# The first mixer of a two-layer network: the keys' decay differences and products on GpSimd, the head mean at the end of the batch's own body, masked scores ahead of the convolution

## The chip, the core and the metric

One core of a Trainium2 chip runs the whole network in one launch. The time is device microseconds (us) from the start of the program to its end. Engines: PE (TensorE), DVE (VectorE), ACT (ScalarE), POOL (GpSimd), SP (SyncE, which issues most loads). They run side by side, each through its own list of instructions in order, and wait for each other by semaphores.

## The reference, cut to the part that changes

The network is a first mixer, a mixture of experts, a second mixer and a feed-forward block, each followed by a residual sum and a layer norm. Only the first mixer changes. It works on 16 batches of 512 rows by 256 columns, with 8 heads:

```python
xc = _causal_dwconv_silu(x, conv_w)                   # 4 taps
q, kg, v, g = xc @ wq, xc @ wkg, xc @ wv, xc @ wg + bg
gk = jax.nn.log_sigmoid(kg) / NORMALIZER              # decay, 128 columns
k = 1.0 - jnp.exp(gk)
o = _gla(qh, kh, vh, gkh, scale)                      # S = S*exp(gk) + k v ; o = q S, step by step
aug_w = jnp.einsum('bhld,hd,bhld->bhl', qh, aug, kh)
o = o + jax.nn.sigmoid(aug_w[..., None] * vh)
o = (o - mu) * jax.lax.rsqrt(var + LN_EPS)            # mean and variance per row and head
return jax.nn.silu(g) * o @ wout                      # then x = layernorm(x + this)
```

## The kernel before

The first mixer is the function `linear_attention`, whose tiles begin with `gla_`; it fills the first 863 us of the span. A batch has 512 positions, cut into 8 chunks of 64 (`NCH`, `CH`) and, inside a chunk, into 8 pieces of 8 (`NSUB`, `SUB`). Channels lie on the 128 partitions. `G` is the decay summed along each chunk (a scan). Within a chunk scores are formed for a piece of queries against all keys up to it, so each chunk needs eight sets of scaled keys: `kt[..., a, 0:n]` with n = 8(a+1). They are made in three steps per a: a difference of `G` (line 787), an exponential on ACT, and a product with `k` (line 805). An instruction takes all 8 chunks, so it has 64, 128, ... 512 elements per partition. `kt` has two buffers, one for each parity of the batch.

The order on each engine is written by hand, in a function `body(b, u, past, more, far)` per engine. While body b finishes batch b, it also does the last steps of batch b-1 (`past`), the front of batch b+1 (`more`) and the convolution of batch b+2 (`far`). Bodies -1, 0 and 1 come first (`starts`), a loop runs bodies 2 to 13 with two bodies in a turn, and bodies 14, 15 and 16 end it (`ends`). On GpSimd, before, a plain loop runs over the 16 batches: a power -1/2 for the head norm (line 726), one for the row norm (line 729), two stores (lines 732 and 735) and a wait for both of them to have landed.

The steps that the text speaks of, by their names in the code:

- `masked(t)` on DVE (lines 816 to 831): takes two chunks' scores from PE through the causal mask into `A`, and carries the state `S` on by two chunks. `outputs(t)` on PE (lines 1115 and 1118) multiplies `S` and `A`; `outputs(t)` on DVE (line 837) adds them to the sigmoid part in `o`. There are four of each in a batch.
- `head_norm(0)` (lines 843 to 845): mean per head, scale, subtraction. `head_norm(1)` (849, 850): variance, from `squares` on ACT (line 954). Then GpSimd's power. `head_norm(2)` (854) multiplies by silu(g), `head_norm(3)` (857) by the power, into `on`.
- `gates` (773 to 775): decay and the scan into `G`. `differences(0)` (782, 783) makes those for `eR` and `khat`. `products(0)` (794 to 800) makes `qt`, `qhat`, `khat`, `aw`.
- `conv(0)` and `conv(1)` (765, 767): the four taps of one half of the channels.
- `tail(0)` (865): `z`, the output projection plus the residual, from the PSUM banks `pV` and `pW`, then its statistics; `tail(1)` (97): the normalized rows `x1`; `tail(2)` (874): the router's logits `lg`.
- On PE `values(t)` (1075, 1076) multiplies the four row tiles by the joint weight of v and g. `values(0)` writes `pV`, which held the output projection, so it waits until both halves of `z` are read. `scores(0)` of batch b+1, near the end of body b, needs all eight `kt`. The order of PE's instructions is the same in both kernels.

## Time and profile before

| | |
|---|---|
| time, median of 3 runs | 4560.33 us (4553.63 to 4561.02) |
| span of the profiled execution | 4569.0 us, 72542 instructions |
| PE busy | 3959.0 us, 87% |
| DVE busy | 2462.4 us, 54% |
| ACT busy | 1991.1 us, 44% |
| POOL busy | 1091.2 us, 24% |

The profile is one execution on its own. Busy shares are averages over the whole network; what the change does is read inside the first 863 us. A row of the trace gives the start in us from the span's beginning, the length in us, engine, line, operation, output and inputs, how many instructions of that form run in a row, and in brackets how long the engine had been idle before it and what ended that. A window row gives the busy time of PE, PE's weight loads, DVE, ACT and POOL in a stretch, the clock granted to PE as a share of full speed, the share of the DMA engines and GB/s.

### The profile page before, as it was taken

How to read it: one execution, taken by the hardware profiler on the slowest of the kernel's cores; microseconds unless marked ns; L12 is line 12 of the kernel's file. 1: busy time of each engine (PE TensorE's matmuls, PEld its weight loads, DVE VectorE, ACT ScalarE, POOL GpSimd, SP SyncE). 2: the span in 40 equal slices, each digit the busy share in tenths (PEclk: the TensorE clock that was granted, in tenths of full speed). 3: DMA queues.
4: the chain of work that ended last, by engine and by line, in shares of the span. 5: the costliest groups of instructions: out<-in, count | busy, mean ns of one | idle time of the engine just before them, and what ended most of it. 6: DMA issues, size and time to landing. Idle time of an engine off the chain costs nothing.

```text
span 4569.0 us, 72542 instructions
## 1 busy us (share of the span) xinstructions
PE 3959.0 (87%) x23860; PEld 3067.1 (67%) x23860; DVE 2462.4 (54%) x5456; ACT 1991.1 (44%) x4069; POOL 1091.2 (24%) x1686
## 2 busy tenths in 40 slices
PE   6888788598999999994688888888888888779998
PEld 3555555377888888882576767666767677656666
DVE  6888888552222222224567777777777776431111
ACT  5655655111222222212466666666666666432221
POOL 0111111101221222213433333333333332200000
PEclk8888889699999999996799999999999999889999
DMA  1010010244555555552111111111111110011111
GB/s 34 29 42 28 28 42 20 72 139 177 184 184 184 184 184 184 184 172 71 46 32 40 42 38 42 43 42 43 42 42 42 43 42 24 19 57 55 55 55 50
DMA packets 220955, 346.96 MB, mean 76 GB/s; under 512 B 99972, under 2 KB 171908, under 8 KB 202500
## 3 DMA queue, kind: packets, MB, share of 16 engines
q1 hardware_dynamic: 196932, 272.74, 18.7%
q0 software_dynamic: 23760, 71.07, 4.9%
q8 instruction: 122, 2.00, 0.2%
q14 instruction: 141, 1.16, 0.1%
HBM read 276.61 MB, written 68.16 MB: 75 GB/s over the span
## 4 chain that ended last, share of the span: by engine, by line
PE 19%; issue 13%; POOL 10%; DVE 5%; ACT 3%; DMA 2%; SPq 2%; POOLq 0%; another core or an unknown queue 0%; DVEq 0%; ACTq 0%
PE gdr_bank L1320 5%; PE gdr_bank L1311 5%; POOL gdr_vblk L1628 2%; POOL gdr_got L1582 2%; POOL gdr_tblk L1626 2%; PE gdr_bank L2358 2%; DVE gdr_y L1729 2%; PE gdr_bank L2329 1%; SPq L1519 1%; PE gdr_bank L2325 1%; PE gdr_bank L2281 1%; POOL gdr_ssq L1616 1%; PE gdr_bank L2341 1%; DMA blocks_in<-gdr_vblk 1%; DMA gdr_T<-blocks_in 1%
## 5 line engine op out<-in xcount | busy, mean ns | idle before, releaser
L525 ACT ACTIVATE moe_rel<-moe_fc 128x512 f32<-128x512 f32 x284 | 169.6, 597 | 798.4 <-PE moe_fc L490 798.4
L490 PE MATMUL moe_fc<-moe_xT,moe_win 128*128 128x256 f32 x2272 | 503.8, 380 | 1.5 <-issue 0.8
L501 PE MATMUL moe_o<-moe_wout,moe_hT 128*128 128x256 f32 x2272 | 502.0, 379 | 0.0
L490 PEld LDWEIGHTS moe_fc<-moe_xT,moe_win 128*128 128x128 f32 x2272 | 432.8, 191 | 61.2 <-issue 2.1
L501 PEld LDWEIGHTS moe_o<-moe_wout,moe_hT 128*128 128x128 f32 x2272 | 426.3, 190 | 55.1
L549 DVE TENSOR_TENSOR moe_hT<-moe_rel 128x512 f32<-128x512 f32 x284 | 196.7, 693 | 361.2 <-ACT moe_rel L525 361.2
L1729 DVE SCALAR_TENSOR_TENSOR gdr_y<-gdr_bank,gdr_cw,gdr_y 128x511 f32<-128x511 f32 (+2 forms) x384 | 287.5, 749 | 82.4 <-ACT gdr_y L1998 63.6
L2206 PE MATMUL gdr_bank<-gdr_hT,gdr_wqkv 128*128 128x512 f32 x512 | 256.9, 626 | 29.6 <-ACT gdr_qk L2013 24.7
L558 DVE COPY moe_osb<-moe_o 128x512 f32<-128x512 f32 x71 | 49.1, 692 | 424.9 <-PE moe_o L501 424.9
L1311 PE MATMUL gdr_bank<-gdr_hT,gdr_wqkv 128*128 128x512 f32 x512 | 224.1, 596 | 3.1 <-ACT gdr_hT L1329 3.1
L1344 DVE TENSOR_TENSOR gdr_kb<-gdr_bank,gdr_x 128x512 f32<-128x512 f32 x32 | 20.6, 686 | 365.1 <-PE gdr_bank L1320 365.1
L2329 PE MATMUL gdr_bank<-gdr_T,gdr_nAT 128*128 128x64 f32 (+1 forms) x1536 | 199.1, 280 | 0.0
L2358 PE MATMUL gdr_bank<-gdr_wo,gdr_y 128*128 128x256 f32 x512 | 156.3, 473 | 48.7 <-ACT gdr_y L2101 48.7
L2325 PE MATMUL gdr_bank<-gdr_ident,gdr_T 128*128 128x128 f32 x768 | 134.4, 304 | 72.6 <-DMA gdr_T<-blocks_in 67.8
L2329 PEld LDWEIGHTS gdr_bank<-gdr_T,gdr_nAT 128*128 128x128 f32 (+1 forms) x1536 | 188.7, 199 | 10.7 <-issue 10.7
L2094 ACT COPY gdr_U<-gdr_bank 128x512 f32<-128x512 f32 x192 | 112.6, 586 | 180.4 <-PE gdr_bank L2325 168.8
L2206 PEld LDWEIGHTS gdr_bank<-gdr_hT,gdr_wqkv 128*128 128x128 f32 x512 | 91.1, 194 | 137.7 <-issue 72.0
L1311 PEld LDWEIGHTS gdr_bank<-gdr_hT,gdr_wqkv 128*128 128x128 f32 x512 | 97.8, 191 | 119.9 <-issue 119.1
L2325 PEld LDWEIGHTS gdr_bank<-gdr_ident,gdr_T 128*128 128x128 f32 x768 | 103.6, 158 | 106.7 <-issue 56.2
L2358 PEld LDWEIGHTS gdr_bank<-gdr_wo,gdr_y 128*128 128x128 f32 x512 | 121.9, 244 | 75.2 <-ACT gdr_y L2101 52.7
L1616 POOL TENSOR_TENSOR gdr_rstd<-gdr_var,gdr_mhalf 128x4 f32<-128x4 f32 x64 | 70.8, 1106 | 419.8 <-DVE gdr_var L91 274.5
L446 POOL COPY moe_ix<-slot_token 128x2 uint32 (+1 forms) x71 | 12.8, 181 | 660.7 <-DMA slots_out<-moe_osb 472.7
(391 smaller groups left out, 8743.7 us busy)
## 6 DMA issues: line engine op xcount, KB each, us to landing
moe_win<-in_moe_w SPq DMA_DIRECT2D x71, 1024.0 KB, 7.8
moe_wout<-in_moe_w SPq DMA_DIRECT2D x71, 1024.0 KB, 5.2
slots_out<-moe_osb POOLq DMA_DIRECT2D x71, 256.0 KB, 7.4
gdr_fz<-mixed_rows SPq DMA_DIRECT2D x18, 512.0 KB, 3.8
gla_xp<-in_xT_rows SPq DMA_DIRECT2D x16, 512.0 KB, 4.6
gla_xres<-in_x_rows SPq DMA_DIRECT2D x16, 512.0 KB, 3.9
token_rows<-gla_x POOLq DMA_DIRECT2D x16, 512.0 KB, 3.4
rt_W<-in_fc_b SPq DMA_DIRECT2D x32, 256.0 KB, 3.4
```

The lines of the kernel that those rows point to most:

```text
L490: ins = nc.tensor.matmul(fc_ps[j][:, m % 2, :], win[u][:, c, m * P:(m + 1) * P], xT[:, c, :], start=(c == 0), stop=(c == DT - 1))
L501: ins = nc.tensor.matmul(o_ps[u][:, t, :], hT[u][:, k, t * P:(t + 1) * P], wout[u][:, k, :], start=(k == 0), stop=(k == FT - 1))
L525: nc.scalar.activation(rel[:, j, :, :], fc_ps[j][:], ACT.Relu).then_inc(relu_done, 1)
L549: nc.vector.tensor_tensor(hT[u][:, 2 * j:2 * j + 2, :], rel[:, j, :, :], rel[:, j, :, :], ALU.mult).then_inc(h_ready, 1)
L1311: ins = nc.tensor.matmul(fc_ps[m % 4][:], win[:, c, m * P:(m + 1) * P], xT[:, c, :], start=(c == 0), stop=(c == DT - 1))
L1320: ins = nc.tensor.matmul(o_ps[t // 2][:, (t % 2) * D:(t % 2 + 1) * D], hT[k][:, t * P:(t + 1) * P], wout[:, k, :], start=(k == 0), stop=(k ...
L1616: nc.gpsimd.tensor_tensor(out, src, mhalf[:, 0:width], ALU.pow).then_inc(s[name], 1)
L1729: ins = stt(y[:, n % 4, d:L], bank[FRONT[n % 2]][:, 0:L - d], cw[:, n, 3 - d:4 - d], y[:, n % 4, d:L], ALU.mult, ALU.add)
L2206: ins = mm(bank[FRONT[n % 2]][:], wqkv[:, c, n * P:(n + 1) * P], hT[:, c, :], start=(c == 0), stop=(c == DT - 1))
L2325: ins = tp(bank[UT][:, h * P:(h + 1) * P], T[:, i, h, :], ident[:])
L2329: ins = mm(bank[YZ[i]][rows_of(lv), h * HP:(h + 1) * HP].rearrange("p (m n) -> p m n", n=half), nAT[:, i, h, rows_of(lv)], first, start=Tr ...
L2358: ins = mm(bank[MIX[p]][:, (t % 2) * D:(t % 2 + 1) * D], y[:, c, tokens(t)], wo_s[:, c, :], start=(c == 0), stop=(c == DH - 1))
```

## The change

Three things are changed in `linear_attention`; what is computed stays the same.

1. The eight `kt` differences and the eight `kt` products of each batch go from DVE to GpSimd (lines 734 and 743 of the new kernel). GpSimd's queue becomes, per body: the power of the head norm of b-1, the eight differences of b+1, the eight products of b+1, the power of the row norm of b-1, the two stores of b-1 and the wait for both to land. New semaphores `G` and `Dk` tell GpSimd that the scan is done, and ACT that a difference is. The scan of a batch waits for the differences of the batch before it (`Dk`), and ACT's exponential of `g` for the products of the batch before it (`kt`).
2. `head_norm(0)` goes from the start of the next body to the end of the batch's own body, after `outputs(3)`; `squares` on ACT goes to the end of the own body too.
3. On DVE `masked(3)` goes ahead of `products` and `z`, `conv(0)` from the body's start to just before `masked(3)`, `gates` behind `outputs(0)`. On ACT the copies of the turned `on` (`turned`) go ahead of the exponentials for `khat`, `gE` and `kt`.

```diff
 # GpSimd
+                def differences(b, u):
+                    wait, _ = waiter(pool, b)
+                    wait("G", 1)
+                    if later(b, 1):
+                        pool.wait_ge(s["sc"], (b - 1) * TT)
+                    for a in range(NSUB):
+                        n, r = SUB * (a + 1), SUB * a + SUB // 2 - 1
+                        nc.gpsimd.tensor_tensor(kt[u][:, :, a, 0:n], G[:, :, r:r + 1].broadcast_to([P, NCH, n]), G[:, :, 0:n],
+                                                ALU.subtract).then_inc(s["Dk"], 1)
+
+                def products(b, u):
+                    wait, _ = waiter(pool, b)
+                    wait("k", 1)
+                    for a in range(NSUB):
+                        n = SUB * (a + 1)
+                        wait("E", 5 + a)
+                        nc.gpsimd.tensor_tensor(kt[u][:, :, a, 0:n], kt[u][:, :, a, 0:n], k_[:, :, 0:n], ALU.mult).then_inc(s["kt"], 1)
...
+                    if past is not None:
+                        head_rstd(past)
+                    if more:
+                        differences(b + 1, w)
+                        products(b + 1, w)
+                    if past is not None:
+                        rows_out(past)
...
 # DVE
-                    Chain(dve, gate_step, b)(v.tensor_tensor_scan(flat(G[:]), flat(notstart[:]), g[:], 0.0, ALU.mult, ALU.add))
+                    if later(b, 0):
+                        dve.wait_ge(s["Dk"], b * NSUB)
+                    done("G", 1, v.tensor_tensor_scan(flat(G[:]), flat(notstart[:]), g[:], 0.0, ALU.mult, ALU.add))
...
                     if past is not None:
-                        head_norm(0, past, w)
+                        head_norm(1, past, w)
+                        head_norm(2, past, w)
...
                         outputs(1, b, u)
                     if far is not None:
                         conv(0, b + 2, u, far)
                     if recur:
+                        masked(3, b, u)
                     if more:
+                        products(b + 1, w)
...
                         outputs(3, b, u)
+                        head_norm(0, b, u)
```

The order of each engine's list shows where the steps went. First DVE, from the scan to the first half of `z` in body 1; in the kernel before, `kt` is made among the rest:

```order
L775 SCALAR_TENSOR_TENSOR gla_G<-gla_notstart,gla_g 128x512
L837 SCALAR_TENSOR_TENSOR gla_o<-gla_sig,gla_pO 128x256
L782 TENSOR_TENSOR gla_eR<-gla_G 128x512
L783 TENSOR_TENSOR gla_khat<-gla_G 128x512
L787 TENSOR_TENSOR gla_kt<-gla_G 128x8x8
L787 TENSOR_TENSOR gla_kt<-gla_G 128x8x16
L787 TENSOR_TENSOR gla_kt<-gla_G 128x8x24
L787 TENSOR_TENSOR gla_kt<-gla_G 128x8x32
L854 TENSOR_TENSOR gla_o<-gla_o,gla_vg 128x1024
L857 TENSOR_TENSOR gla_on<-gla_o,gla_rstd 128x1024
```

In the changed kernel the same place, DVE from the last step of `masked(2)`'s state to `qt`; the four rows from L800 on are `conv(0)` and the start of `masked(3)`:

```order
L857 SCALAR_TENSOR_TENSOR gla_S<-gla_S,gla_gE,gla_kvm 128x256 x2
L863 SCALAR_TENSOR_TENSOR gla_o<-gla_sig,gla_pO 128x256
L800 TENSOR_SCALAR gla_yc<-gla_xp,gla_conv_w 128x512
L802 SCALAR_TENSOR_TENSOR gla_yc<-gla_xp,gla_conv_w,gla_yc 128x512 x3
L844 MEMSET gla_hold 128x1
L845 COPY_PREDICATED gla_A<-gla_causal,gla_pU 128x512
L853 TENSOR_TENSOR gla_kvm<-gla_pKV,gla_blockmask 128x256
L857 SCALAR_TENSOR_TENSOR gla_S<-gla_S,gla_gE,gla_kvm 128x256
L825 TENSOR_TENSOR gla_qt<-gla_eR,gla_q 128x512
```

The `kt` rows are gone from DVE, and `conv(0)` with `masked(3)` now lies between `outputs(1)` and the products that `z` comes behind. Next POOL, one batch of the loop before:

```order
L726 TENSOR_TENSOR gla_rstd<-gla_var,gla_mhalf 128x32
L729 TENSOR_TENSOR gla_rstd<-gla_var,gla_mhalf 128x4
L732 ISA
L732 DMA token_rows<-gla_x 128x4x256
L735 ISA
L735 DMA router_logits<-gla_lg 128x4x8
```

And POOL in the changed kernel, the end of body 1, from the largest differences to the stores (`token_rows` is the output of `x1`):

```order
L734 TENSOR_TENSOR gla_kt<-gla_G 128x8x56
L734 TENSOR_TENSOR gla_kt<-gla_G 128x8x64
L743 TENSOR_TENSOR gla_kt<-gla_kt,gla_k 128x8x8
L743 TENSOR_TENSOR gla_kt<-gla_kt,gla_k 128x8x16
L743 TENSOR_TENSOR gla_kt<-gla_kt,gla_k 128x8x24
L743 TENSOR_TENSOR gla_kt<-gla_kt,gla_k 128x8x32
L743 TENSOR_TENSOR gla_kt<-gla_kt,gla_k 128x8x40
L743 TENSOR_TENSOR gla_kt<-gla_kt,gla_k 128x8x48
L743 TENSOR_TENSOR gla_kt<-gla_kt,gla_k 128x8x56
L743 TENSOR_TENSOR gla_kt<-gla_kt,gla_k 128x8x64
L750 TENSOR_TENSOR gla_rstd<-gla_var,gla_mhalf 128x4
L752 DMA token_rows<-gla_x 128x4x256
```

Sixteen instructions now stand between GpSimd's two powers. Last, DVE at the end of a body in the changed kernel; before, `L843` to `L845` came as the first three instructions of the next body, behind `lg`:

```order
L863 SCALAR_TENSOR_TENSOR gla_o<-gla_sig,gla_pO 128x256
L869 TENSOR_REDUCE gla_mu<-gla_o 128x32
L870 TENSOR_SCALAR gla_mu<-gla_mu 128x32
L871 TENSOR_TENSOR gla_o<-gla_o,gla_mu 128x1024
L836 COPY gla_augw<-gla_pB 128x32
L839 TENSOR_TENSOR gla_sig<-gla_vg,gla_augw 128x1024
```

The mean of the own batch now stands between its last output and the `augw` and `sig` of the next batch.

## Rows read from the trace of the kernel before

**Rows 1.** Windows of one body: busy PE, PEld, DVE, ACT, POOL; clock; DMA share, GB/s.

```profile
447.56:476.49 28.93, 18.77 (x236) 14.68 (x236) 26.38 (x42) 19.44 (x31) 5.45 (x1) 0.76 0.00 1
476.49:489.98 13.49, 13.43 (x74) 6.57 (x75) 11.76 (x33) 6.18 (x11) 1.82 (x2) 1.00 0.34 117
489.98:495.05 5.07, 5.07 (x62) 4.64 (x62) 4.09 (x9) 3.98 (x4) 0.00 (x0) 1.00 0.00 0
```

**Rows 2.** The window of the loop, bodies 2 to 13.

```profile
149.61:740.90 591.29, 483.30 (x4513) 322.95 (x4512) 506.71 (x984) 355.07 (x528) 96.31 (x48) 0.88 0.10 32
```

**Rows 3.** Timeline, the two handovers of that body: PE's first values, DVE's last output.

```profile
476.55 1.98 PE L1075 MATMUL gla_pV<-gla_wvg,gla_xc 128*128 128x512 f32 x4 [0.46 <-DVE gla_z L865]
...
489.98 0.42 DVE L837 SCALAR_TENSOR_TENSOR gla_o<-gla_sig,gla_pO 128x256 f32<-128x256 f32 x1 [0.32 <-PE gla_pO L1118]
```

**Rows 4.** Timeline of DVE in the same body: the steps that the change moves.

```profile
447.56 1.22 DVE L843 TENSOR_REDUCE gla_mu<-gla_o 128x32 f32<-128x1024 f32 x1 [3.17 <-issue]
...
450.50 0.49 DVE L765 TENSOR_SCALAR gla_yc<-gla_xp,gla_conv_w 128x512 f32<-128x512 f32 x1 [0.25 <-DVE gla_o L845]
451.03 2.33 DVE L767 SCALAR_TENSOR_TENSOR gla_yc<-gla_xp,gla_conv_w,gla_yc 128x512 f32<-128x512 f32 x3
...
462.05 1.40 DVE L787 TENSOR_TENSOR gla_kt<-gla_G 128x64 f32<-128x64 f32 x4
...
466.00 2.47 DVE L787 TENSOR_TENSOR gla_kt<-gla_G 128x320 f32<-128x320 f32 x4
...
478.49 1.67 DVE L805 TENSOR_TENSOR gla_kt<-gla_kt,gla_k 128x64 f32<-128x64 f32 x4
...
481.73 0.06 DVE L818 MEMSET gla_hold<- 128x1 f32 x1 [0.15 <-DVE gla_x L97]
...
483.48 0.42 DVE L837 SCALAR_TENSOR_TENSOR gla_o<-gla_sig,gla_pO 128x256 f32<-128x256 f32 x1
484.03 2.74 DVE L805 TENSOR_TENSOR gla_kt<-gla_kt,gla_k 128x320 f32<-128x320 f32 x4
...
490.92 0.19 DVE L810 COPY gla_augw<-gla_pB 128x32 f32<-128x32 f32 x1 [0.52 <-PE gla_pB L1145]
```

**Rows 5.** GpSimd's elementwise work in the second mixer: two groups (count, min/median/max ns; count, busy us, mean ns).

```profile
L1623 POOL TENSOR_TENSOR gdr_vblk<-gdr_vblk,gdr_id x32: 716/718/726, 2186.9 to 3991.5; 64x256 f32<-64x256 f32 x32
...
L1628 POOL TENSOR_TENSOR gdr_vblk<-gdr_vblk,gdr_tblk 64x56 f32<-64x56 f32 x64 | 19.2, 300 | 5.0
```

**Rows 6.** Timeline, DVE beside GpSimd: second mixer, then the first mixer's power.

```profile
2365.13 0.30 POOL L1628 TENSOR_TENSOR gdr_vblk<-gdr_vblk,gdr_tblk 64x56 f32<-64x56 f32 x1
2365.24 0.23 DVE L1770 SCALAR_TENSOR_TENSOR gdr_sp<-gdr_sp,gdr_t 128x16 f32<-128x16 f32 x1
...
2365.50 0.17 DVE L1771 TENSOR_TENSOR gdr_sp<-gdr_sp,gdr_nexpA 128x16 f32<-128x16 f32 x1
...
2365.71 1.22 DVE L1776 TENSOR_TENSOR gdr_kb<-gdr_qk,gdr_bt 128x1024 f32<-128x1024 f32 x1
2365.90 1.20 POOL L1628 TENSOR_TENSOR gdr_vblk<-gdr_vblk,gdr_tblk 64x54 f32<-64x54 f32 x1
...
457.56 5.45 POOL L726 TENSOR_TENSOR gla_rstd<-gla_var,gla_mhalf 128x32 f32<-128x32 f32 x1 [11.77 <-DVE gla_var L850]
...
458.70 1.23 DVE L775 TENSOR_TENSOR_SCAN gla_G<-gla_notstart,gla_g 128x512 f32<-128x512 f32 x1
```

**Rows 7.** Windows for PE's clock: an idle stretch, the work behind it, the first values.

```profile
456.15:460.71 4.56, 0.00 (x2) 0.03 (x1) 4.17 (x7) 1.93 (x3) 3.15 (x1) 0.58 0.00 0
460.71:470.50 9.79, 7.20 (x77) 5.80 (x78) 9.19 (x16) 7.45 (x15) 2.30 (x1) 0.50 0.00 1
...
48.46:57.50 9.04, 9.04 (x11) 3.32 (x12) 1.92 (x3) 2.31 (x4) 0.00 (x0) 0.50 0.21 58
```

**Rows 8.** Timeline of POOL in body 16, the last: store of batch 14, power of batch 15.

```profile
826.64 0.76 POOL L735 DMA_DIRECT2D router_logits<-gla_lg  x1 [8.32 <-DVE gla_lg L874]
831.50 6.49 POOL L726 TENSOR_TENSOR gla_rstd<-gla_var,gla_mhalf 128x32 f32<-128x32 f32 x1 [4.09 <-DVE gla_var L850]
```

More of the change, by code:

```diff
@@ L739, in _, with body @@
                     pool.nop().then_inc(lg_free, 1)
+                def body(b, u, past, more, far):
+                    w = 1 - u
+                    if past is not None:
[5 more added lines that the diff above has]
+                        rows_out(past)
+                starts(body)
+                with pool.Fori(0, (B - 4) // 2) as i:
+                    for u in range(2):
+                        body(i * 2 + 2 + u, u, i * 2 + 1 + u, True, i + 2)
+                ends(body)
             @block.vector
@@ L789, in products @@
[L789 to L805 removed]
+                    ref8 = blocks8(G[:])[:, :, SUB // 2 - 1:SUB // 2].broadcast_to([P, NCH * NSUB, SUB])
@@ new lines, in differences, with products @@
+                    done("D", 1, tt(blocks8(eR[:]), blocks8(G[:]), ref8, ALU.subtract))
+                    done("D", 2, tt(khat[:], G[:, :, CH - 1:CH].broadcast_to([P, NCH, CH]), G[:], ALU.subtract))
+                def products(b, u):
+                    wait, done = waiter(dve, b)
+                    wait("q", 1)
+                    wait("E", 1)
+                    done("qt", 1, tt(qt[:], flat(eR[:]), qs[:], ALU.mult))
+                    wait("E", 2)
+                    done("qhat", 1, tt(qhat[u][:], flat(eG[:]), qs[:], ALU.mult))
+                    wait("k", 1)
+                    wait("E", 3)
+                    done("khat", 1, tt(khat[:], khat[:], k_[:], ALU.mult))
+                    done("aw", 1, tt(aw[:], qs[:], flat(k_[:]), ALU.mult))
@@ L878, in body @@
                     if past is not None:
-                        head_norm(0, past, w)
+                        head_norm(1, past, w)
+                        head_norm(2, past, w)
+                    if recur:
+                        masked(1, b, u)
+                        outputs(0, b, u)
+                    if more:
+                        gates(b + 1)
+                        differences(b + 1)
+                    if past is not None:
+                        head_norm(3, past, w)
+                    if recur:
+                        masked(2, b, u)
+                        outputs(1, b, u)
                     if far is not None:
@@ L909, in body @@
                     if recur:
-                        masked(3, b, u)
-                        outputs(2, b, u)
-                    if more:
-                        products(2, b + 1, w)
-                    if far is not None:
-                        conv(1, b + 2, u, far)
-                    if recur:
                         outputs(3, b, u)
+                        head_norm(0, b, u)
                     if more:
@@ L968, in exponents @@
                     else:
-                        for a in range(4 * (part - 1), 4 * part):
+                        for a in range(NSUB):
                             n = SUB * (a + 1)
-                            wait("D", 3 + a)
+                            wait("Dk", a + 1)
                             done("E", 5 + a, a_op(kt[u][:, :, a, 0:n], kt[u][:, :, a, 0:n], ACT.Exp))
```

79 lines of the change are left out of this document (20 added, 59 removed).

## The prediction

> **What bounds the kernel now.** I read the slices of the span first: the first mixer is its first fifth, and nothing else changes. Then I cut one body of the loop at the instants where one engine hands the path to another. Twelve bodies take 591.29 us, 49.27 each [rows 2]. In the body from 447.56 to 495.05 there are three stretches [rows 1]. In A, from the head mean to the second half of `z`, 28.93 us, DVE is busy 26.38 and PE only 18.77: DVE sets the length. At its end PE has waited 0.46 us for `z` and starts `values` [rows 3]. In B, 13.49 us, PE is busy 13.43: PE sets it, and at its end DVE takes its last `outputs` 0.32 us after PE's sums [rows 3]. In C, 5.07 us, DVE goes from that to `lg`; 0.52 of it is a wait for PE's `augw` sums [rows 4]. Behind C the next body's A begins. At every second body the loop's turn adds 3.17 us of idle DVE [rows 4], 1.6 a body. The sum, 28.93 + 13.49 + 5.07 + 1.6 = 49.1, is the measured 49.27 within 0.2, so a body is A + B + C, and a microsecond taken from DVE in B is worth nothing while PE is full there.
>
> I forecast the difference that the change makes on the profiled execution, whose span is 4569.0 us, and add it to the median of the runs, 4560.3: the span lies 9 us above it, and that the two differ does not bear on a difference of one part.
>
> **A, without any conflict between engines.** The head mean leaves: 450.50 - 447.56 = 2.94 us. The eight differences leave: 1.40 + 2.47 = 3.87. `masked(3)` comes in, from 481.73 to 483.48: 1.75 [all rows 4]. `conv(0)` moves within A. `gates` and the head norm's steps change places within A. A' = 28.93 - 2.94 - 3.87 + 1.75 = 23.9. The eight products on DVE, 1.67 + 2.74 = 4.41 us [rows 4], lie in B, where PE is full; taking them away is worth nothing.
>
> **GpSimd's new work.** No row shows GpSimd on these shapes. Elementwise work of two SBUF operands takes it 0.717 us for 256 elements and 0.300 for 56 [rows 5]: 2.1 ns an element and 0.18 fixed. Sixteen instructions with 2 x 2304 elements are 9.7 us of elements and 2.9 fixed, 12.6 us against 8.3 on DVE. They start when `G` is there, about 8.5 us into the body: the power takes 5.45 [rows 6] and can't start before the stores of the body before have landed, some 3 us in, so power and scan end together. The products end some 25 us in even with conflicts; `scores(0)`, which needs them, is late in B, some 43 in. So 18 us are spare, and neither `kt` nor the second power, some 5 us behind `z`, holds PE. If GpSimd took twice as long, `kt` would still be in time. The moved exponentials on ACT have the same slack. The new wait of the scan on `Dk` is for work that ended half a body earlier: nothing.
>
> **What GpSimd does to DVE.** This is the disputed term. In the second mixer an elementwise GpSimd instruction that begins 0.19 us after a DVE instruction with two SBUF operands takes 1.20 us instead of 0.30: it ends when DVE's 1.22 us are over. The other way round, a small DVE instruction that begins under a GpSimd read of 0.30 takes 0.23 instead of 0.17 and ends 0.04 after it [rows 5, 6]. So the two wait for each other, whoever came first. But under the power, 5.45 us long, the scan runs at 1.23 us [rows 6], so that instruction does not hold DVE for its length. The new instructions are of the first kind, only longer: 0.13 to 1.08 us of elements. I walk DVE's order after the scan past them. A DVE instruction with two SBUF operands waits for what is left of the read that runs. `on` and the two states of `masked(2)` lose 0.8 together; the convolution's four taps 1.1; the state of `masked(3)` 0.4; `qt`, `qhat` and `khat`, which meet the largest products, 0.6, 0.7 and 0.8. With small ones that is 4.5 us a body, an estimate from rows 5. Instructions with a PSUM operand I count as free. The ends: 0, if a long read lets DVE through as the power does; 9.7, if DVE waits for all of GpSimd's elements. I take 4.5, since rows 6 show DVE held by the same operation. A' = 23.9 + 4.5 = 28.4, 0.5 less than before.
>
> The Trainium skill, "SBUF — State Buffer", section "Who interferes with whom", says that a DVE instruction with two SBUF inputs contends with a GpSimd instruction that reads SBUF, and that who issues first has the shared pair for the whole instruction. The short pairs above agree (1.20 for 0.30, 0.23 for 0.17). The power does not: by the page's words it would hold DVE for 5.45 us, and the new place of the power, beside the first half of A, would then cost up to some 4 us a body more, a total near 4660.
>
> **B.** PE's instructions are the same, but PE now waits longer ahead of `values`. What PE has between `masked(2)` and `values` (the scores, the output projection, `outputs(2)`) ended 0.46 us before `z` did. In front of `z` DVE now has in addition `conv(0)`, 0.49 + 2.33, and `masked(3)`, 1.75 [rows 4]: PE idles 0.46 + 4.6 = 5.0 us without conflicts, and some 3.6 of the 4.5 us of waits fall there: 8.7. The rows on what follows an idle PE: idle for 4.56 us, after which the clock is 0.50 for 9.79 us, and in the first batch, after a wait, 9.04 us of full work on `values` at 0.50 [rows 7]; the granted clock is 1.2 instead of 2.4 GHz. In B it was 1.00 [rows 1]. Full work of 9.04 us at half clock loses about half, 4.5 us; a clock that stays up loses 0. I take the middle, 2.2, since the slow stretch can begin while PE is still idle. B' = 15.7.
>
> **C.** The head mean comes in, 2.94, ahead of `augw`, so that the wait of 0.52 for PE's sums goes under it. C' = 5.07 + 2.94 - 0.52 = 7.5. `squares` on ACT now run beside `augw` and `masked(0)` of DVE, and the variance at the start of the next body finds them done.
>
> **The sum.** A body: -0.5 + 2.2 + 2.4 = +4.1. Bodies 1 to 13 do it: 13 x 4.1 = 53. Body 14 has no convolution and so less waiting: +1. The filling, with `kt` of batch 0 on the slower engine, is covered by `values`: +1. In body 16 the power of the last batch but none started at 831.50, and took 6.49 us for it ran beside DVE's product; now it waits only for the store issued at 826.64 to land, some 2 us behind its issue [rows 8]: 2.4 earlier and 1 shorter, 3.5; the same in body 15, so -7. Total 53 + 1 + 1 - 7 = +48: **4608 us**.
>
> **The rivals.**
>
> *DVE is not held by long GpSimd reads; faster* (the other side). For it: the scan under the power [rows 6]. Against: the short pair. A body is then 23.9 + 15.7 + 7.5 against 47.5: -0.4 with the clock still lost, 13 x -0.4 - 7 + 1 = -11, 4549. It decides at the point where DVE's waits fall under 0.8 us a body: each microsecond of wait is worth 13.
>
> *The same, and the clock ahead of `values` is kept,* since PE then idles only 5 us: -2.6 a body, 13 x -2.6 - 6 = -40, 4520.
>
> *DVE waits between 0.2 and 1.5 us a body:* 13 times that less 11, within 9 us of no change, 4560.
>
> *DVE is held in full,* or nearly: 7 to 9.7 us of waits, and 4.5 for the clock. With 8 us and 2.2 it is 13 x 7.6 - 5 = +94, 4654.
>
> *That GpSimd is too slow for `scores(0)`* needs over 40 us for 12.6 of work; I give it nothing of its own. That the change doesn't do what it says is not open: the order shows the sixteen instructions on GpSimd.
>
> **Chances.** The forecast, waits of 1.5 to 7 us: 0.53. Not held, clock lost: 0.16. Not held, clock kept: 0.10. Between: 0.13. Held in full: 0.08. A measurement of this kernel can tell about 0.2%, 9 us, from no change. Faster: 0.16 + 0.10 = 0.26. Same: 0.13. Slower: 0.53 + 0.08 = 0.61. The range leaves out the kept clock (0.10) and most of the full hold (0.08): its low end, 4538, lies under the not held case with a little of the clock back; its high end, 4655, is the forecast with 6 us of waits and the clock's upper end, 13 x (1.5 + 2.3) = 49 more. The forecast's own range is 4572 to 4655.
>
> **What would show it.** In the profile after: DVE rows of `qt`, `qhat` and `khat` that were 0.69 us long should be 1.2 to 1.5 and end with GpSimd's products; at 0.69 the first rival holds. GpSimd's differences should take 0.3 to 1.3 us each, more under DVE. PE's first `values` should have some 9 us of idle time ahead of it, ended by `z`, and take 3.8 us for its four matmuls instead of 1.98; 1.98 means that the clock was kept. The way from DVE's last `outputs` to `lg` should be 7.5 us. `scores(0)` should not wait for `kt`. The loop should take 53.4 us a body. The prediction is wrong if the windows of A come out under 24 or over 31 us, or if GpSimd becomes what PE waits for.

## The result and the profile after

The changed kernel took 4579.99 us (median of 6 runs, 4570.33 to 4585.48) against 4556.79 of the kernel before (6 runs). The ratio is 1.0055, with a 95% interval from 1.0041 to 1.0068: 19 to 31 us slower. The forecast was 48 us slower with a range of 4538 to 4655. The sign and the range held; the size was double what came.

The profiled execution of the changed kernel has a span of 4580.7 us. Its first mixer ends later by 29.7 us: the last `lg` starts at 890.2 instead of 860.5. What follows is the same program in both, and took 3690.5 us here and 3708.5 in the profile before; in the other profiles of this study it took 3683 to 3717. So the two spans differ by 11.7 us only because of the part that did not change, and the first mixer's own 29.7 agrees with the 19 to 31 of the timed runs.

Two bodies of the loop, each cut as in [rows 1] into A, B and C, and then the loop and the end, correspond to [rows 1] and [rows 2]. The columns are those of [rows 1]; the first A here contains the loop's turn.

```profile
469.02:497.80 28.78, 18.88 (x239) 14.41 (x237) 25.70 (x35) 19.24 (x31) 21.84 (x18) 0.80 0.01 1
497.80:515.69 17.89, 17.83 (x74) 7.96 (x75) 6.41 (x21) 5.31 (x10) 1.83 (x2) 0.74 0.25 88
515.69:522.98 7.29, 7.29 (x67) 5.66 (x67) 6.73 (x12) 5.04 (x5) 0.00 (x0) 1.00 0.00 0
523.01:550.77 27.76, 17.88 (x239) 13.65 (x237) 25.69 (x35) 19.39 (x31) 22.36 (x18) 0.89 0.01 1
550.77:566.18 15.41, 15.36 (x74) 7.19 (x75) 6.41 (x21) 5.16 (x9) 1.83 (x2) 0.87 0.29 102
...
156.77:781.66 624.89, 502.91 (x4514) 324.03 (x4513) 466.02 (x793) 355.03 (x528) 287.14 (x240) 0.86 0.09 30
781.66:893.00 111.34, 77.32 (x715) 57.34 (x713) 59.80 (x122) 34.27 (x52) 40.03 (x29) 0.77 0.08 25
```

A body takes 624.89 / 12 = 52.07 us instead of 49.27. In B the granted clock is 0.74 and 0.87, where it was 1.00, and PE is busy with the same 74 instructions for 17.83 and 15.36 us instead of 13.43. DVE is busy only 6.41 us of B.

The timeline of DVE in the second of these bodies, then its wait for PE at the end of the first one's B:

```profile
535.90 2.19 DVE L857 SCALAR_TENSOR_TENSOR gla_S<-gla_S,gla_gE,gla_kvm 128x256 f32<-128x256 f32 x2
...
539.33 2.62 DVE L802 SCALAR_TENSOR_TENSOR gla_yc<-gla_xp,gla_conv_w,gla_yc 128x512 f32<-128x512 f32 x3
...
543.84 1.27 DVE L825 TENSOR_TENSOR gla_qt<-gla_eR,gla_q 128x512 f32<-128x512 f32 x1
545.23 1.41 DVE L827 TENSOR_TENSOR gla_qhat<-gla_eG,gla_q 128x512 f32<-128x512 f32 x1
546.76 1.55 DVE L830 TENSOR_TENSOR gla_khat<-gla_khat,gla_k 128x512 f32<-128x512 f32 x1
...
515.69 0.42 DVE L863 SCALAR_TENSOR_TENSOR gla_o<-gla_sig,gla_pO 128x256 f32<-128x256 f32 x1 [11.19 <-PE gla_pO L1138]
```

`qt`, `qhat` and `khat` were 0.69 us each before, the two states 1.01, the three taps 2.33. With 0.22 on the first tap and 0.09 on `on` they are longer by 3.94 us a body. GpSimd's two sets beside them, and PE's first `values` after the idle stretch, in the first of these two bodies and in the one ahead of it:

```profile
531.61 7.40 POOL L734 TENSOR_TENSOR gla_kt<-gla_G 128x64 f32<-128x64 f32 x8 [0.19 <-DVE gla_G L812]
538.97 8.80 POOL L743 TENSOR_TENSOR gla_kt<-gla_kt,gla_k 128x64 f32<-128x64 f32 x8
...
444.45 3.78 PE L1095 MATMUL gla_pV<-gla_wvg,gla_xc 128*128 128x512 f32 x4 [7.10 <-DVE gla_z L891]
...
497.86 3.78 PE L1095 MATMUL gla_pV<-gla_wvg,gla_xc 128*128 128x512 f32 x4 [6.40 <-DVE gla_z L891]
```

The products end 24.8 us into the body, and nothing waits for `kt`. PE stands still ahead of `values` for 7.10 and 6.40 us in these rows, 6.4 to 7.4 over the loop, instead of 0.46 [rows 3], and its first four matmuls take 3.78 us instead of 1.98. The kind of all this is as the prediction had it; PE's idle time was given as some 9 us. Two things of A are not in it at all. Before, DVE waited 0.97 to 1.21 us for `squares` in each body that doesn't begin behind a turn of the loop, and each turn cost it 2.9 to 3.2 us ([rows 4] show one of 3.17). The six turns of two bodies hold five such returns, so this is 5 of the 12 bodies. This row of the kernel before is in the body after the one that [rows 1] show; the one of the changed kernel is the first row of DVE behind a turn:

```profile
504.57 1.22 DVE L849 TENSOR_REDUCE gla_var<-gla_sq 128x32 f32<-128x1024 f32 x1 [1.20 <-ACT gla_sq L954]
```

```profile
469.56 1.22 DVE L875 TENSOR_REDUCE gla_var<-gla_sq 128x32 f32<-128x1024 f32 x1 [0.54 <-DVE gla_lg L900]
```

The wait for `squares` is gone, and the turn costs 0.54 to 0.57.

### The profile page after: what moved, and what is told of

Same layout as the page of the kernel before. It is cut to its first block, busy times and chain, and to the rows that moved or that the text cites. A ratio compares the mean times of both kernels' runs of the same rounds, so it can differ in the third digit from the quotient of the medians.

```text
span 4580.7 us, 72189 instructions
## 1 busy us (share of the span) xinstructions
PE 3973.5 (87%) x23860; PEld 3062.5 (67%) x23860; DVE 2408.3 (53%) x5200; ACT 1991.4 (43%) x4069; POOL 1346.5 (29%) x1942
## 4 chain that ended last, share of the span: by engine, by line
PE 21%; issue 11%; POOL 9%; DVE 6%; ACT 3%; DMA 2%; SPq 1%; POOLq 0%; DVEq 0%; ACTq 0%
PE gdr_bank L1340 5%; PE gdr_bank L1331 5%; POOL gdr_vblk L1648 2%; DVE gdr_y L1749 2%; POOL gdr_got L1602 2%; POOL gdr_tblk L1646 2%; PE gdr_bank L2378 2%; PE gdr_bank L2349 1%; PE gdr_bank L2345 1%; SPq L1539 1%; PE gdr_bank L2361 1%; PE gdr_bank L2301 1%; PE gdr_bank L2226 1%; POOL gdr_ssq L1636 1%; DMA blocks_in<-gdr_vblk 1%
## 5 line engine op out<-in xcount | busy, mean ns | idle before, releaser
L2226 PE MATMUL gdr_bank<-gdr_hT,gdr_wqkv 128*128 128x512 f32 x512 | 260.6, 634 | 28.5 <-ACT gdr_qk L2033 24.9
L1095 PE MATMUL gla_pV<-gla_wvg,gla_xc 128*128 128x512 f32 x128 | 91.4, 854 | 98.6 <-DVE gla_z L891 92.0
```

The costliest lines, as they stand in the source:

```text
L2226: ins = mm(bank[FRONT[n % 2]][:], wqkv[:, c, n * P:(n + 1) * P], hT[:, c, :], start=(c == 0), stop=(c == DT - 1))
```

## The experiments

Every kernel was cut in the same way, from the end of one `lg` to the end of the next: A to the end of the second half of `z` (with the turn of the loop in every second body), B to the start of DVE's last `outputs`, C to the end of `lg`; the 0.03 us from there to DVE's next record are in the body alone. The columns are means over bodies 2 to 13 in us, the start of the last `lg`, the median of the runs, and its ratio to the kernel before in runs on the same chip, with the 95% interval.

| kernel | A | B | C | body | last `lg` | median | ratio |
|---|---|---|---|---|---|---|---|
| before | 30.71 | 13.48 | 5.04 | 49.27 | 860.5 | 4556.8 | |
| changed | 28.24 | 16.51 | 7.29 | 52.07 | 890.2 | 4580.0 | 1.0055 (1.0041 to 1.0068) |
| e1_short_gp | 24.42 | 16.95 | 7.29 | 48.69 | 843.0 | 4524.5 | 0.9932 (0.9908 to 0.9956) |
| e2_z_first | 21.39 | 13.87 | 7.36 | 42.66 | 762.9 | 4454.1 | 0.9783 (0.9767 to 0.9800) |
| e3_warm | 29.89 | 17.06 | 7.28 | 54.27 | 923.6 | 4646.3 | 1.0203 (1.0171 to 1.0236) |
| e4_on_dve | 29.51 | 15.54 | 7.30 | 52.39 | 894.1 | 4590.9 | 1.0089 (1.0072 to 1.0106) |
| e5_nops | 28.24 | 16.52 | 7.28 | 52.08 | 891.2 | 4578.8 | 1.0061 (1.0042 to 1.0080) |
| e6_warm6 | 28.25 | 13.89 | 7.29 | 49.46 | 858.7 | 4548.5 | 0.9997 (0.9981 to 1.0012) |
| e7_gp_only | 27.56 | 13.93 | 5.11 | 46.64 | 819.2 | 4516.8 | 0.9922 (0.9899 to 0.9945) |
| e8_mean_back | 28.44 | 14.25 | 5.04 | 47.77 | 837.8 | 4530.8 | 0.9960 (0.9945 to 0.9975) |
| e9_on_early | 21.32 | 15.51 | 7.36 | 44.22 | 780.8 | 4467.7 | 0.9817 (0.9794 to 0.9841) |
| e10_zfirst_dve | 26.02 | 16.13 | 7.32 | 49.50 | 855.1 | 4546.8 | 0.9984 (0.9969 to 0.9999) |
| e11_long_list | 29.29 | 15.88 | 7.47 | 52.67 | 898.0 | 4588.7 | 1.0075 (1.0052 to 1.0098) |
| e12_conv_behind | 25.02 | 16.00 | 7.29 | 48.34 | 841.5 | 4521.5 | 0.9926 (0.9903 to 0.9948) |

The theory was the prediction's: GpSimd's reads hold DVE, and what stands ahead of `z` starves PE until its clock falls. The rival was that GpSimd's part costs nothing and the order alone does, or the other way round.

### e1_short_gp: GpSimd's instructions made short

```diff
-                        n, r = SUB * (a + 1), SUB * a + SUB // 2 - 1
+                        n, r = SUB, SUB * a + SUB // 2 - 1
...
-                        n = SUB * (a + 1)
+                        n = SUB
...
-                            done("E", 5 + a, a_op(kt[u][:, :, a, 0:n], kt[u][:, :, a, 0:n], ACT.Exp))
+                            done("E", 5 + a, a_op(kt[u][:, :, a, 0:n], G[:, :, 0:n], ACT.Exp))
```

> The changed kernel with GpSimd's sixteen instructions cut to 8 columns of each chunk (64 elements each); the exponentials for kt read G instead, so seven eighths of the keys' differences and products are left out. Order, waits and counts of instructions stay. Theory (DVE is held by GpSimd's reads): S, conv, qt, qhat and khat on DVE fall back to their lengths of before; A goes from 28.2 to some 24.3 us a body, PE's idle time ahead of values from 6.4 to 7.1 to some 4, B to between 13.5 and 16.5, C stays 7.3. 52 to 91 us less than the changed kernel. Rival (the holding does not lie on the path, the order of the moved steps costs the time): under 13 us less.

DVE's products and PE's first `values` in one body:

```profile
421.40 0.82 DVE L825 TENSOR_TENSOR gla_qt<-gla_eR,gla_q 128x512 f32<-128x512 f32 x1
422.34 0.69 DVE L827 TENSOR_TENSOR gla_qhat<-gla_eG,gla_q 128x512 f32<-128x512 f32 x1
423.16 0.69 DVE L830 TENSOR_TENSOR gla_khat<-gla_khat,gla_k 128x512 f32<-128x512 f32 x1
...
426.36 3.15 PE L1095 MATMUL gla_pV<-gla_wvg,gla_xc 128*128 128x512 f32 x4 [3.52 <-DVE gla_z L891]
```

The same sixteen instructions, only shorter, leave DVE's at 0.69, and A falls by 3.8 us, as said: the length of GpSimd's reads is what held DVE. The kernel is 1.2 points faster than the changed one, 56 us, at the low end of 52 to 91, because B did not fall. PE still idles 2.3 to 3.6 us ahead of `values`, and B is 14.9 to 19.8 us. With an idle stretch half as long the clock still falls in every body.

### e2_z_first: the convolution and the masked scores behind z

```diff
                         outputs(1, b, u)
-                    if far is not None:
-                        conv(0, b + 2, u, far)
-                    if recur:
-                        masked(3, b, u)
                     if more:
                         products(b + 1, w)
                     if past is not None:
                         tail(0, past)
                     if recur:
+                        masked(3, b, u)
                         outputs(2, b, u)
-                    if far is not None:
-                        conv(1, b + 2, u, far)
                     if past is not None:
                         tail(1, past)
+                    if far is not None:
+                        conv(0, b + 2, u, far)
+                        conv(1, b + 2, u, far)
```

> The changed kernel with conv(0) and masked(3) on DVE put behind z (z's statistics, masked(3), outputs(2), x1, conv(0), conv(1), outputs(3)). Theory (PE starves ahead of values because conv(0) and masked(3) stand in front of z, and its clock falls): A 28.2 - 4.6 - 0.5 = 23.1, PE's idle time ahead of values under 2 us, B 13.5 with its four first matmuls at 1.98 us, C 7.3: 8 us a body, some 105 less than the changed kernel, some 80 under the kernel before. Rival (the clock is lost anyhow, from the idle time further ahead in A): A as said, B 16.5: 65 less. Rival (DVE becomes late for the last outputs in B, with 11.2 us of work there): B over 14.5 with the clock full.

PE in one body, and DVE's last output in the same:

```profile
453.15 1.11 PE L1143 MATMUL gla_pA<-gla_ident,gla_on 128*128 128x128 f32 x4 [2.97 <-DVE gla_on L883]
...
463.86 1.98 PE L1093 MATMUL gla_pV<-gla_wvg,gla_xc 128*128 128x512 f32 x4
...
477.29 0.42 DVE L863 SCALAR_TENSOR_TENSOR gla_o<-gla_sig,gla_pO 128x256 f32<-128x256 f32 x1 [2.20 <-PE gla_pO L1136]
```

At most 0.3 us of idle time stand ahead of `values` now, its matmuls take 1.98, and the body is 9.4 us shorter than that of the changed kernel; the theory said 8. Of the 9.4, 2.6 are B's and 6.9 are A's, where 5.1 had been expected: DVE's rows that meet GpSimd's reads are also longer by only 1.5 us a body instead of 3.9 (`qhat` is back at 0.69). The ratio is 0.9783: 98 us faster than the kernel before. This version beats both. All that the change moved to GpSimd and all that it moved into C is still in it; two steps stand behind `z` instead of ahead of it (and `x1` ahead of `conv(1)`).

### e3_warm and e6_warm6: PE kept busy ahead of values

```diff
                         outputs(2, b, u)
+                    if recur and more and past is not None:
+                        for _ in range(12):
+                            mm(pA[:], ident[:], xc[:, 0, :], start=True, stop=True)
                     if more:
                         values(0, b + 1)
```

> The changed kernel with twelve matmuls of 128x512 into the free bank pA on PE between outputs(2) and values, whose results are overwritten: 12 x 0.5 = 6 us at full clock in an idle stretch of 6.4 to 7.1. Theory (B is longer by the lost clock alone): B 16.5 to 13.5 us, A and C unchanged, 3.0 us a body, 39 less than the changed kernel. Rival (B is longer because of what comes late for it, as khat or aw): B stays over 15.5, under 13 less.

I had taken one matmul of 128x512 at 0.5 us; the twelve took 10.57, so they reached past the idle stretch and held `values` up:

```profile
508.77 10.57 PE L1225 MATMUL gla_pA<-gla_xc,gla_ident 128*128 128x512 f32 x24
519.17 1.88 PE L1095 MATMUL gla_pV<-gla_wvg,gla_xc 128*128 128x512 f32 x4
```

`values` ran at full clock, but the kernel lost 66 us on the changed one. It was done again with `range(6)`:

> As e3_warm with six matmuls of 128x512 into pA instead of twelve: by e3_warm's trace (10.57 us for twelve) they take 5.3 us, inside PE's idle stretch of 6.4 to 7.1. Theory (B is longer by the lost clock alone): B 16.5 to 13.5 or 14 us, A and C unchanged, 2.5 to 3 us a body, 32 to 39 less than the changed kernel. Rival (as in e3_warm PE's longer list makes PE's loop turn dear, 3 to 4 us at each second body): half of that gain is lost again, 10 to 20 less.

```profile
423.38 5.42 PE L1225 MATMUL gla_pA<-gla_xc,gla_ident 128*128 128x512 f32 x12
...
430.49 1.98 PE L1095 MATMUL gla_pV<-gla_wvg,gla_xc 128*128 128x512 f32 x4 [1.69 <-DVE gla_z L891]
...
480.06 3.58 PE L1095 MATMUL gla_pV<-gla_wvg,gla_xc 128*128 128x512 f32 x4 [2.03 <-DVE gla_z L891]
```

B is 13.89 us instead of 16.51, A and C are the same to 0.01, and the ratio falls from 1.0055 to 0.9997, by 31.5 us in the medians (32 to 39 were expected). In nine of the twelve bodies B is 13.48, as before the change; in the other three, like that of the last row, `values` are slow again and B is 15.13. So the whole lengthening of B is the lost clock, and it makes up all that the changed kernel loses on the kernel before. Work that is thrown away brings most of it back. PE's dearer turn, the rival's half of the gain, came with twelve matmuls and not with six (below).

### e4_on_dve and e10_zfirst_dve: the keys' work back on DVE

In both, the differences stand on DVE behind `head_norm(3)` and the products behind the last step ahead of `outputs(3)`; GpSimd's sixteen instructions are gone. The first has the changed kernel's order, the second that of e2_z_first.

```diff
 # GpSimd
-                    if more:
-                        differences(b + 1, w)
-                        products(b + 1, w)
...
 # DVE
                         head_norm(3, past, w)
+                    if more:
+                        kt_differences(b + 1, w)
...
+                    if more:
+                        kt_products(b + 1, w)
                     if recur:
                         outputs(3, b, u)
```

> The changed kernel with the kt differences and products back on DVE: differences behind head_norm(3), products behind x1. The other moves stay. Theory (GpSimd's reads take from DVE in A what the differences gave back): A 28.2 - 3.9 + 3.9 = 28.2, so A is the same; PE's idle time ahead of values falls by the waits that stood there to some 4 to 5 us; B 13.5 to 16.5. 0 to 39 less than the changed kernel. Rival (the move to GpSimd is a gain and the other moves are what costs): 3.9 us more in A, some 50 more than the changed kernel.

> e2_z_first with the kt differences and products back on DVE: differences behind head_norm(3), products behind conv(1). Theory (with z early, GpSimd's part is a gain because DVE is nearly full in B): A 21.4 + 3.9 - 1.8 (waits for GpSimd that go) = 23.5, B set by DVE, 11.2 + 4.4 = 15.6 against 13.9, DVE's turn 1.4 dearer: 5 us a body, 60 to 70 more than e2_z_first. Rival (GpSimd's part is worth nothing here as in e4_on_dve): within 10 of e2_z_first.

In the changed kernel's order A is 27.73 us in the bodies without a turn, against 27.76 with GpSimd: DVE's 3.9 us of differences and its 3.9 us of waits cost A the same. In the bodies with a turn it is 31.8 instead of 28.75. The row behind the turn says why:

```profile
473.85 1.22 DVE L885 TENSOR_REDUCE gla_var<-gla_sq 128x32 f32<-128x1024 f32 x1 [3.65 <-issue]
```

B was 1 us shorter on the mean; PE's idle time ahead of `values` was 2.5 to 5.6 us. The ratio of 1.0089 is some 15 us above the changed kernel's 1.0055, neither the expected gain nor the rival's 50. With `z` early it is another matter: e10_zfirst_dve lies 93 us above e2_z_first, more than the 60 to 70 expected. B is 16.1 and was expected at 15.6; A is 26.0 and was expected at 23.5, and what else lengthens it has not been followed. Its products on DVE come when PE waits for them:

```profile
481.17 4.53 DVE L841 TENSOR_TENSOR gla_kt<-gla_kt,gla_k 128x64 f32<-128x64 f32 x8
485.74 0.42 DVE L873 SCALAR_TENSOR_TENSOR gla_o<-gla_sig,gla_pO 128x256 f32<-128x256 f32 x1
...
485.84 1.15 PE L1121 MATMUL gla_pU<-gla_qspread,gla_kt 128*64 128x64 f32 x32 [1.24 <-DVE gla_kt L841]
```

DVE's last output has no idle time ahead of it: DVE sets B now. So the value of GpSimd's part depends on the order around it: 0.3 us a body where PE starves ahead of B anyhow, 7 us where DVE is full.

### e5_nops and e11_long_list: a longer list for DVE's loop

Between two turns the trace holds 315 records of DVE's list in the kernel before, 294 in e4_on_dve and 230 in the changed kernel; from the turn's branch to the next record pass 2.7 to 2.9, 3.1 to 3.4 and 0.3 us. The first trial put forty empty instructions in each body, ahead of `outputs(3)`:

```diff
+                        for _ in range(40):
+                            dve.nop()
                         outputs(3, b, u)
```

> The changed kernel with forty empty instructions in each body of DVE, ahead of outputs(3), where DVE is idle for over 10 us. Between two turns of DVE's loop the trace of the changed kernel holds 230 of DVE's records, that of before 315, and after the turn's branch DVE stands still 0.3 us here and 2.7 to 2.9 there. Theory (a longer list of DVE's instructions makes the turn dear): 2.5 to 3 us idle at the turn come back, 6 turns, 12 to 20 us more than the changed kernel. Rival (the turn was dear before for what ran ahead of it, not for the length): turn 0.3 us, under 4 more.

The trace still has 230 records between two turns, and the body is the same to 0.01. Whether the empty instructions stand in the list without a record the trace doesn't show, so this run decides nothing. The second put 36 memsets of one column each there:

```diff
+                        for i in range(36):
+                            v.memset(pad[:, i:i + 1], 0.0)
                         outputs(3, b, u)
```

> As e5_nops, whose empty instructions left no records (230 between two turns there too), with 36 memsets of one column in each body of DVE ahead of outputs(3), some 2.2 us in an idle stretch of over 10. Some 300 records between two turns. Theory (the list's length makes DVE's turn dear): 2.5 to 3 us after the branch, A of every second body from 28.75 to 31.5, 12 to 20 us more than the changed kernel. Rival (the turn's price has another cause): 0.3 us after the branch, A 28.75.

```profile
476.60 1.22 DVE L876 TENSOR_REDUCE gla_var<-gla_sq 128x32 f32<-128x1024 f32 x1 [3.08 <-issue]
```

With 302 records the turn costs 3.08 us again, and A in the bodies with a turn goes from 28.75 to 31.3. The theory holds for the turn, with the list's length counted in records of the trace. The body grew by only 0.6 us on the mean and the ratio by 0.2 points, some 9 us, and not 12 to 20: B lost less to the clock in the bodies with a dear turn (15.0 and 15.6 against 15.3 and 17.9). Why it did, I have not tried.

### e7_gp_only: GpSimd's part with the order of before

```diff
 # DVE
                     if past is not None:
-                        head_norm(1, past, w)
-                        head_norm(2, past, w)
+                        head_norm(0, past, w)
+                    if far is not None:
+                        conv(0, b + 2, u, far)
...
-                    if far is not None:
-                        conv(0, b + 2, u, far)
-                    if recur:
-                        masked(3, b, u)
                     if more:
                         products(b + 1, w)
                     if past is not None:
                         tail(0, past)
+                        tail(1, past)
                     if recur:
+                        masked(3, b, u)
                         outputs(2, b, u)
...
                         outputs(3, b, u)
-                        head_norm(0, b, u)
```

`squares` goes back with the mean; the new place of `turned` on ACT stays.

> The kept part is the kt differences and products on GpSimd; on DVE the order of before comes back (head mean and squares in the next body, conv(0) at the body's start, masked(3) behind z and x1). Theory (GpSimd's part alone, in an order that leaves z early, is a small gain): A 30.7 of before - 3.9 (differences) + 3 to 4 (waits for GpSimd) - 1.35 (turn) = 28.5 to 29.5, B 13.5, C 5.0, body 47 to 48 against 49.27, 15 to 30 us less than the kernel before. Rival (the waits on qt, qhat, khat starve PE ahead of values and its clock falls): B 15 or more, within 10 of the kernel before.

```profile
448.01 1.34 DVE L827 TENSOR_TENSOR gla_qhat<-gla_eG,gla_q 128x512 f32<-128x512 f32 x1
...
452.83 1.98 PE L1096 MATMUL gla_pV<-gla_wvg,gla_xc 128*128 128x512 f32 x4
```

`qhat` is held as in the changed kernel, but PE reaches `values` without a pause and at full clock. A body takes 46.64 us, 2.6 less than before, and the ratio is 0.9922, 36 us, a little over the 15 to 30 expected. A is 27.56 and not 28.5 to 29.5: in this order DVE's rows beside GpSimd are longer by only 1.4 us a body instead of the 3 to 4 expected. GpSimd's part alone is a gain; about 1 of the 2.6 us is the cheaper turn (0.5 instead of 2.9 to 3.2 in 5 of 12 bodies).

### e8_mean_back: the head mean back in the next body

```diff
+                    if past is not None:
+                        head_norm(0, past, w)
+                    if recur:
+                        masked(1, b, u)
                     if past is not None:
                         head_norm(1, past, w)
                         head_norm(2, past, w)
...
                         outputs(3, b, u)
-                        head_norm(0, b, u)
```

This is on top of e2_z_first.

> e2_z_first with the head mean and the squares back in the next body (mean first, then masked(1), then the variance). Theory (the mean costs C what it gives A, and the wait for the squares comes on top): C 7.36 to 5.0, A 21.4 to 24.3 or 25: 0.6 to 1.3 us a body, 8 to 17 more than e2_z_first. Rival (in e2_z_first PE sets the body from on onward, and on comes 2.9 us later): as much more, with PE's idle time ahead of the turned on at 6 us and a lower clock behind it, over 25 more. Rival (the mean in C was a loss by itself): less than e2_z_first.

```profile
440.36 1.22 DVE L875 TENSOR_REDUCE gla_var<-gla_sq 128x32 f32<-128x1024 f32 x1 [2.44 <-ACT gla_sq L971]
...
441.83 1.23 DVE L880 TENSOR_TENSOR gla_o<-gla_o,gla_vg 128x1024 f32<-128x1024 f32 x1
...
441.88 6.49 POOL L725 TENSOR_TENSOR gla_rstd<-gla_var,gla_mhalf 128x32 f32<-128x32 f32 x1 [9.69 <-DVE gla_var L876]
...
448.47 1.24 DVE L883 TENSOR_TENSOR gla_on<-gla_o,gla_rstd 128x1024 f32<-128x1024 f32 x1 [0.70 <-POOL gla_rstd L725]
449.76 1.12 PE L1145 MATMUL gla_pA<-gla_ident,gla_on 128*128 128x128 f32 x4 [3.91 <-DVE gla_on L883]
```

A body is 5.1 us longer than in e2_z_first; the theory's 0.6 to 1.3 was far too little, and the first rival holds in its size (77 us), if not in its idle time (3.9 us and not 6). Mean, squares, variance and the power are a chain that ends in `on`, and `on` starts 17.1 to 17.6 us behind the body's first instruction instead of 9.9 or 10.1. The power takes 6.49 us here and not 5.45, in every body: DVE's product with two SBUF operands began 0.05 us ahead of it. Moving the mean into the own body costs C 2.25 us and takes that chain off A.

### e9_on_early: the head norm's last step ahead of two differences

```diff
                         gates(b + 1)
-                        differences(b + 1)
                     if past is not None:
                         head_norm(3, past, w)
+                    if more:
+                        differences(b + 1)
```

This is on top of e2_z_first.

> e2_z_first with head_norm(3) on DVE ahead of the differences for eR and khat, right behind the scan. In e2_z_first PE stands still 2.97 us for on and then runs without a pause to the end of the body. Theory (on sets PE's restart and PE the rest): on starts 1.45 us earlier, PE's idle time falls to 1.5 us, 1.2 to 1.5 us a body, 15 to 20 less than e2_z_first. Rival (the power's end is as late as the differences' end, or z waits for qt, qhat, khat that come later now): under 6 less.

```profile
461.39 0.65 PE L1144 MATMUL gla_pA<-gla_ident,gla_on 128*128 128x128 f32 x4 [1.47 <-DVE gla_on L883]
...
472.65 3.30 PE L1094 MATMUL gla_pV<-gla_wvg,gla_xc 128*128 128x512 f32 x4 [2.32 <-DVE gla_z L891]
```

PE's idle time for `on` fell to 1.47 as said, and PE arrived earlier at `values`, where it now waits 2.32 us for the same `z`. The clock falls at the start of B in ten of the twelve bodies, and B is 15.51 on the mean instead of 13.87. The kernel lost 14 us on e2_z_first. The idle time had been moved from light work to the front of PE's densest stretch. That `z` would be no earlier was in the rival; that this costs more than it gives was in neither.

### e12_conv_behind: only the convolution behind z

```diff
-                    if far is not None:
-                        conv(0, b + 2, u, far)
                     if recur:
                         masked(3, b, u)
...
                     if far is not None:
+                        conv(0, b + 2, u, far)
                         conv(1, b + 2, u, far)
```

> The changed kernel with conv(0) alone put behind z and outputs(2); masked(3) stays ahead of the products. Theory (what stands ahead of z counts by its length, the clock falls with the idle time): A 28.2 - 2.9 - 0.5 = 24.9 to 25.0, PE's idle time ahead of values 3 to 4 us, B 13.5 to 15.5: 45.7 to 47.8 a body against 52.07 and 42.66 for e2_z_first, 55 to 80 less than the changed kernel. Rival (the convolution alone was the loss): as e2_z_first within 10. Rival (masked(3) alone was): within 15 of the changed kernel less 3.4 a body, 40 less.

```profile
466.03 3.78 PE L1094 MATMUL gla_pV<-gla_wvg,gla_xc 128*128 128x512 f32 x4 [3.04 <-DVE gla_z L891]
...
516.01 3.68 PE L1094 MATMUL gla_pV<-gla_wvg,gla_xc 128*128 128x512 f32 x4 [4.11 <-DVE gla_z L891]
```

A is 25.02 as said, and PE's idle time 3 to 4 us as said, but B is 16.00, over the 13.5 to 15.5 expected. With the shorter of the two steps alone ahead of `z`, 1.75 of 4.6 us, B still loses 2.5 us to the clock of the 3.0 that the changed kernel loses. The body is 48.34, and the kernel took some 58 us less than the changed one, as the theory had it (55 to 80). The remaining 1.75 us of `masked(3)` are worth 5.7 more in e2_z_first, which also has `x1` ahead of `conv(1)`; the place of `x1` was not tried alone.

## Why the prediction was right in sign and wrong in size

Its terms against what the profile shows, in us (a body is a body of the loop):

| term | forecast | measured |
|---|---|---|
| A | -0.5 | -2.47 |
| B | +2.2 | +3.03 |
| C | +2.4 | +2.25 |
| a body | +4.1 | +2.80 |
| 12 bodies of the loop | +49 | +33.6 |
| bodies -1 to 1 | +5 | +7.0 |
| body 14 | +1 | -3.4 |
| bodies 15 and 16 | -7 | -7.5 |
| first mixer | +48 | +29.7 |

**The step that failed is A**, put at -0.5 and measured at -2.47. "At every second body the loop's turn adds 3.17 us of idle DVE" was put into the sum before and carried over unchanged. The turn costs 0.54 to 0.57 us after the change, some 2.5 less, in 5 of the 12 bodies: 1.05 on the mean. e11_long_list shows that the list's length decides it: nothing but instructions were added, and 3.08 us came back. The Trainium skill, "Runtime: NRT & Kernel Launch", section "Instruction fetch mechanics", says that a taken branch whose target is not in the current window of two pages (a page is a block of 256 instructions) has to fetch it first. The runs agree in kind, with 2.7 to 3.5 us at 293 to 315 records of DVE's list and 0.2 to 0.3 at 229 to 235; where between 235 and 293 it turns, no run shows. The prediction said that taking the eight products off DVE, behind PE, "is worth nothing"; they are half of the sixteen instructions that shorten the list, and how much of the turn is due to them no run shows either. In the whole body the dear turn was worth less than in A, 0.6 us on the mean in e11_long_list, since B lost less there.

The second part of the same failure is the body that was read. [rows 1] are a body behind a turn. In the seven that don't begin behind one DVE waited 0.97 to 1.21 us for `squares`, which the turn covers in the one that I read; this wait went too, 0.7 on the mean. GpSimd's waits were 3.94 us instead of 4.5, another 0.6. These three make 2.3 where 2.0 are missing; the rest, small gaps the other way, I have not followed.

**B** had the right mechanism, which e6_warm6 shows alone, and a size too small by 0.8, although PE idled 6.4 to 7.4 us and not the 8.7 of the prediction's sum. The middle between none and the row of 9.04 us at half clock [rows 7] was a choice without a row behind it. The bodies' B lie between 15.3 and 17.9 us, inside the 13.5 to 18.0 that its bounds allow.

**C** was right, and so were the length and end of GpSimd's work, that nothing waits for `kt`, and the end of the mixer. **Body 14** has no convolution at all, and it became 3.4 us faster, not 1 slower: B grew by 1.7 and C by 2.1, but A fell by 7.2. Before, DVE waited in its A 2.35 us for `squares` and 1.48 us for PE's scores; after, for neither. The bodies -1 to 1 are read from the first `lg`, 156.6 instead of 149.6.

**The disputed term** was decided for the forecast: e1_short_gp shows that DVE waits for the length of GpSimd's reads, and the rival that long reads let DVE through falls. The power is an exception on one side, as rows of both kernels show: DVE runs beside it at its usual length, but a DVE product that began ahead of it holds it (e8_mean_back). But the waits were not why the change lost. They only eat up what the differences give (e4_on_dve), and without them and with the changed order the clock is lost all the same (e1_short_gp). C's 2.25 are the head mean, which A gave up. The loss that is left is B, and B is the order ahead of `z` (e2_z_first, e12_conv_behind).

**What the prediction did not ask** is what the three parts are worth apart. With `z` early, GpSimd's part is worth 93 us (e10_zfirst_dve against e2_z_first) and the mean in the own body 77 (e8_mean_back against e2_z_first). The third part, `conv(0)` and `masked(3)` ahead of `z`, takes some 125 from the two (e2_z_first against the changed kernel): 6.9 us a body in A, which DVE's steps ahead of `z` fill, and 2.6 in B by the clock.

## What to carry to other kernels

Where two engines pass the path to and fro, ask of each step in front of a handover whether the other engine waits behind it: 4.6 us of DVE's work that nobody waited for, put in front of the step that releases PE, cost more than all that was won elsewhere. Of the 9.4 us a body that it cost here, 6.9 are the longer way to that step, with the waits for GpSimd on it, and 2.6 are PE's idle time come back as a low clock in the work behind it. Read more than one body before you write down a cycle, and both kinds where a loop is unrolled by two. A change that makes a loop's list of instructions shorter or longer can change what the loop's turn costs.

## What the runs showed of the hardware

- DVE's loop turn costs 0.2 to 0.3 us from the branch with 229 to 235 records of its list between two turns, and 2.7 to 3.5 with 293 to 315. PE's turn went the same way in e3_warm: with 871 weight loads between two turns PE stood still at the turn and its clock fell, with 847 (e6_warm6) and 823 (the changed kernel) not.

```profile
481.59 3.78 PE L1084 MATMUL gla_pA<-gla_xc,gla_wq 128*128 128x512 f32 x4 [1.93 <-issue]
```

- A GpSimd elementwise instruction holds a DVE instruction with two SBUF operands for what is left of it: `khat` 1.55 instead of 0.69 us beside GpSimd's product of 512 elements. The power on GpSimd, 5.45 us, holds none that begins under it; it takes 6.49 us itself when DVE's product of 1.23 us with two SBUF operands began 0.05 us ahead of it (e8_mean_back).
- GpSimd's own sixteen instructions take 15.7 to 16.2 us beside DVE's work (7.40 and 8.80 in the rows above), and 14.6 in e7_gp_only, where fewer of DVE's instructions meet them, against 12.6 estimated from rows of undisturbed ones.
- PE's clock: an idle stretch ahead of `values` of 6.4 to 7.4 us (changed kernel), of 3.0 to 4.1 (e12_conv_behind), and also of 2.03 (e6_warm6) and 1.52 (e9_on_early) was followed by slow `values`, 3.2 to 3.8 us for the first four matmuls in most bodies, and one of 2.49 (e4_on_dve), of 1.69 (e6_warm6) or none was not (1.98). So the length of the stretch alone doesn't decide it; what PE did ahead of it I have not tried apart.

```profile
502.25 1.98 PE L1109 MATMUL gla_pV<-gla_wvg,gla_xc 128*128 128x512 f32 x4 [2.49 <-DVE gla_z L901]
...
206.56 3.45 PE L1094 MATMUL gla_pV<-gla_wvg,gla_xc 128*128 128x512 f32 x4 [1.52 <-DVE gla_z L891]
```

The first row is of e4_on_dve, the second of e9_on_early.
